# One-hot batches between the halves of the projections, expert tiles from pair 1, an eighth pair in 18 of 67 tiles

## What is computed

```python
xn = layernorm(x)
# state space: y = layernorm(xn)*gamma+beta; left, right = split(y @ W_up + b_up)
# left = silu(causal_conv3(left)); delta = softplus(left @ W_delta + b)
def step(h, inputs):
    u_t, d_t, b_t, c_t = inputs
    dA = jnp.exp(d_t[..., None] * A)
    h = dA * h + (d_t * u_t)[..., None] * b_t[:, None, :]
    y = jnp.einsum('bdn,bn->bd', h, c_t)
    return (h, y)
# s = xn + ((y + u*D) * silu(right)) @ W_down + b_down
# experts: the two best of 8 by xn @ gate, softmax over the two
# eo = (silu(xn @ w1) * (xn @ w3)) @ w2        (256 -> 1024 -> 256, for each expert)
# f = sum of the two experts' eo, weighted
out = x + s * silu(f)
```

## Time and profile before

| | us |
|---|---|
| runs | 1358.0, 1359.04, 1367.18; median 1359.04 |
| profiled execution | 1357.34, of which span 1355.5 |
| PE busy | 1189.3 (88%) |
| DVE busy | 1164.6 (86%) |
| POOL busy | 1076.8 (79%) |
| ACT busy | 756.1 (56%) |

### The profile page before, as it was taken

One profiled execution on the slowest core, in us unless ns is written; L12 is line 12 of the kernel. 1 busy time (PEld: TensorE's weight loads), 2 busy tenths in 40 slices (PEclk: granted clock), 3 DMA queues, 4 the chain that ended last, 5 costly groups with the idle time before them and its releaser, 6 DMA issues.

```text
span 1355.5 us, 26186 instructions
## 1 busy us (share of the span) xinstructions
PE 1189.3 (88%) x7740; PEld 916.5 (68%) x7740; DVE 1164.6 (86%) x1668; ACT 756.1 (56%) x1619; POOL 1076.8 (79%) x1044
## 2 busy tenths in 40 slices
PE   6767789999999999999889998999899989997850
PEld 5435577877777777777667876777687767775410
DVE  7726889989799888999888987998898979998988
ACT  3752475556655675566645664557555665555532
POOL 0032689889999889889988987899998888988974
PEclk7899799999999999999999999999999999997555
DMA  7114345564556545743474437444854476455658
GB/s 230 49 39 140 104 127 170 146 217 131 142 158 187 176 129 163 235 132 128 142 233 135 136 119 239 139 136 129 241 154 128 132 217 171 139 169 179 191 180 279
DMA packets 124319, 216.55 MB, mean 160 GB/s; under 512 B 15040, under 2 KB 40768, under 8 KB 124160
## 3 DMA queue, kind: packets, MB, share of 16 engines
q10 hardware_dynamic: 73728, 134.25, 34.0%
q1 hardware_dynamic: 43616, 61.83, 13.9%
q0 software_dynamic: 6816, 18.62, 4.3%
HBM read 190.67 MB, written 23.99 MB: 158 GB/s over the span
## 4 chain that ended last, share of the span: by engine, by line
PE 69%; POOL 9%; issue 8%; DMA 6%; DVE 5%; ACT 2%; SPq 0%; POOLq 0%; ACTq 0%; DVEq 0%
PE bank L1311 32%; PE bank L1281 15%; PE bank L1259 7%; PE bank L1325 7%; POOL arena L434 5%; DMA wring<-in_w_all 4%; PE bank L1166 2%; POOL hid L449 2%; PE bank L1188 1%; PE bank L1294 1%; PE bank L1196 1%; DVE arena L863 1%; PE bank L1268 1%; DVE xn L872 1%; DMA xg<-xn_d,source 1%
## 5 line engine op out<-in xcount | busy, mean ns | idle before, releaser
L434 POOL TENSOR_TENSOR arena<-arena,c_rep 128x512 f32<-128x512 f32 x512 | 604.2, 1185 | 113.0 <-DVE arena L1036 103.9
L1036 DVE TENSOR_TENSOR_SCAN arena<-bank,carry,arena 128x512 f32<-128x512 f32 x512 | 651.9, 1273 | 22.2 <-ACT bank L799 21.9
L1311 PEld LDWEIGHTS bank<-xgT,wring 128*128 128x128 f32 x4288 | 515.8, 193 | 134.9 <-issue 104.9
L1311 PE MATMUL bank<-xgT,wring 128*128 128x128 f32 x4288 | 536.3, 279 | 49.2 <-issue 29.0
L799 ACT ACTIVATE bank<-arena,a_neg 128x512 f32<-128x512 f32 x512 | 354.2, 692 | 122.1 <-DVE arena L1036 43.2
L1027 DVE TENSOR_TENSOR arena<-bank,b_rep 128x512 f32<-128x512 f32 x512 | 351.3, 686 | 32.5 <-PE bank L1325 11.2
L714 ACT ACTIVATE th<-bank 128x256 f32<-128x256 f32 x284 | 108.9, 384 | 339.0 <-PE bank L1311 303.9
L1325 PE MATMUL bank<-stack,pick 128*128 128x512 f32 x512 | 281.0, 550 | 17.0 <-DVE arena L1027 16.9
L1281 PE MATMUL bank<-wring,hid 128*128 128x256 f32 x1072 | 271.3, 386 | 8.6 <-POOL hid L449 8.5
L1281 PEld LDWEIGHTS bank<-wring,hid 128*128 128x128 f32 x1072 | 195.7, 191 | 63.1 <-issue 22.0
L449 POOL TENSOR_TENSOR hid<-gt,ue 128x256 f32<-128x256 f32 x284 | 207.0, 729 | 12.9 <-DVE gt L1048 12.7
(11 more groups left out here) (180 smaller groups left out, 772.9 us busy)
## 6 DMA issues: line engine op xcount, KB each, us to landing
arena<-delta_d ACTq DMA_DIRECT2D x512, 256.0 KB
wring<-in_w_all SPq DMA_DIRECT2D x64, 384.0 KB, 5.2
xn<-in_x SPq DMA_DIRECT2D x4, 1024.0 KB, 9.8
xn_d<-xn SPq DMA_DIRECT2D x4, 1024.0 KB, 5.5
parts_d<-spare SPq DMA_DIRECT2D x16, 256.0 KB
stack<-parts_d SPq DMA_DIRECT2D x16, 256.0 KB, 5.7
wring<-results SPq DMA_DIRECT2D x8, 512.0 KB, 9.1
arena<-results SPq DMA_DIRECT2D x8, 512.0 KB, 7.7
```

The lines of the kernel that those rows point to most:

```text
L434: pool.tensor_tensor(p_ring[:, s % P_RING, :], h_ring[:, s % H_RING, :], of_chunk(c_rep, c, 2), ALU.mult).then_inc(s_hc, 1)
L1036: v.tensor_tensor_scan(out=h_ring[:, s % H_RING, :], data0=a_bank[s % 2][:, :], data1=b_ring[:, s % B_RING, :], initial=carry[:, q:q + 1], ...
L1311: ins = pe.matmul(bank[:, m * SW + r * SLOT:m * SW + (r + 1) * SLOT], wring[:, 2 * j + r, (2 * m + h) * P:(2 * m + h + 1) * P], xgT[:, i % ...
```

## The change

The full batches and the shared ones are chosen by the list `SHARED` instead of every second; the batches are placed between and behind the two halves of each projection, from chunk 3 on, all of them before chunk 6 (batches 0 to 2 stand behind the products of chunk 0); transposes go one chunk ahead, and ACT's order follows. The destinations, the first gather and the first weight loads (in two parts) go ahead of the pairs. `yh`'s ring is turned round, so that the weights of the first four slots fit behind the rows that are used up first. Tiles start at pair 1; `EXTRA` spreads 18 pairs over the 67 live tiles; dead tiles take four pairs. They now stand at pairs 488 to 503.

```diff
-MOE_FIRST = 5
-PLACED_AT, GATHER_AT, WEIGHTS_AT = 1, 2, 1
+MOE_FIRST = 1
+SHARED = (1, 5, 7, 9, 11, 13, 15)
-LONG, SHORT = 7, 5
+LONG, SHORT, EXTRA = 7, 4, 18
...
-        first = MOE_FIRST + LONG * min(i, LONG_TILES) + SHORT * max(i - LONG_TILES, 0)
+        full = min(i, LONG_TILES)
+        first = MOE_FIRST + LONG * full + EXTRA * full // LONG_TILES + SHORT * (i - full)
...
+        def yh_row(c):
+            return (YH_RING - 1 - c % YH_RING) * TC
...
             load_stack(0)
+            sp.wait_ge(s_table, 1)
+            sp.wait_ge(s_ytr, YH_RING)
+            load_weights(0, (0, 1))
+            sp.wait_ge(s_ytr, NC)
+            load_weights(0, (2, 3))
...
-                if s == WEIGHTS_AT:
-                    sp.wait_ge(s_ytr, NC)
-                    sp.wait_ge(s_table, 1)
-                    load_weights(0, range(STEPS))
...
             gate_of_right(0)
+            pool.wait_ge(s_slot, 1)
+            values_of_halves(SHARED[0])
             for part in range(4):
                 delta_sum(0, part)
             low_part(0)
-            pool.wait_ge(s_slot, 1)
-            for b in range(1, BATCHES, 2):
+            for b in SHARED[1:]:
                 values_of_halves(b)
+            pool.wait_ge(s_placed, 5)
+            pool.wait_ge(s_xst, 16 * 4)
+            gather_rows(0)
...
+            evict_columns(3)
             evict_halves(2)
-            evict_columns(3)
             evict_c(0)
             scale_rows(4)
             high_part(0)
+            evict_columns(4)
+            scale_rows(5)
             evict_halves(3)
-            evict_columns(4)
-            for c in range(5, NC):
-                scale_rows(c)
-                evict_halves(c - 1)
-                evict_columns(c)
-            evict_halves(NC - 1)
+            for c in range(4, NC):
+                if c + 1 < NC:
+                    evict_columns(c + 1)
+                if c + 2 < NC:
+                    scale_rows(c + 2)
+                evict_halves(c)
...
-                if b % 2 == 0:
+                if b not in SHARED:
...
-            for b in range(BATCHES // 2):
+            for b in range(2):
                 one_hots(b)
...
-            for b in range(BATCHES // 2, BATCHES):
+            for b in range(2, BATCHES):
                 one_hots(b)
+            placed()
...
-            def left_right(c):
+            def left_right(c, between=()):
...
+                    if m == 0:
+                        for b in between:
+                            place_batch(b)
...
             product(0, "b")
+            place_batch(0)
             transpose_y(3)
             product(0, "c")
-            left_right(3)
-            placed_to = 0
-            for c in range(4, NC):
-                transpose_y(c)
-                left_right(c)
-                for b in range(placed_to, min(placed_to + 3, BATCHES)):
+            place_batch(1)
+            place_batch(2)
+            placed_to = 3
+            for c in range(3, NC):
+                if c + 1 < NC:
+                    transpose_y(c + 1)
+                left_right(c, range(placed_to, min(placed_to + 2, BATCHES)))
+                upto = min(placed_to + (5 if c == 5 else 4), BATCHES)
+                for b in range(placed_to + 2, upto):
                     place_batch(b)
-                placed_to += 3
-            for b in range(placed_to, BATCHES):
-                place_batch(b)
+                placed_to = upto
...
+                if s == 0:
+                    pe.wait_ge(s_lrev, NC - 1)
```

More of the change, by code:

```diff
@@ L410, in values_of_halves @@
             def values_of_halves(b):
-                pool.wait_ge(s_equal, b // 2 + 1)
+                pool.wait_ge(s_equal, SHARED.index(b) + 1)
                 shape = [P, BATCH, TILES]
@@ L415, in values_of_halves @@
                 pool.tensor_tensor(goals, weights, blocks(goal, b).unsqueeze(2).broadcast_to(shape), ALU.mult).then_inc(s_val, 1)
-                pool.wait_ge(s_val, 2 * (b // 2) + 1)
+                pool.wait_ge(s_val, 2 * SHARED.index(b) + 1)
                 pool.tensor_tensor(weights, weights, blocks(prob, b).unsqueeze(2).broadcast_to(shape), ALU.mult).then_inc(s_val, 1)
@@ L527, in _ @@
                     after_outs(BY_PAIR[s - 2])
-                if s == GATHER_AT:
-                    pool.wait_ge(s_placed, 5)
-                    pool.wait_ge(s_xst, 16 * 4)
-                    gather_rows(0)
                 for name, c, r in WORK[s]:
@@ L609, in scale_rows @@
                 for n in range(c * TC, (c + 1) * TC):
-                    ins = act.activation(yh[:, n % (YH_RING * TC), :], xn[:, n, :], ACT.Identity, scale=rs2[:, n:n + 1])
+                    ins = act.activation(yh[:, yh_row(c) + n % TC, :], xn[:, n, :], ACT.Identity, scale=rs2[:, n:n + 1])
                 ins.then_inc(s_yh, 1)
@@ L1069, in _ @@
                     gates(BY_PAIR[s - 1])
-                if s == PLACED_AT:
-                    placed()
                 c, at = s // PAIRS, s % PAIRS
@@ L1153, in transpose_y @@
                     pe.wait_ge(s_yev, c)
-                transpose_chunk(yh, (c % YH_RING) * TC, banks[0:2]).then_inc(s_ytr, 1)
-            def left_right(c):
+                transpose_chunk(yh, yh_row(c), banks[0:2]).then_inc(s_ytr, 1)
+            def left_right(c, between=()):
                 pe.wait_ge(s_yev, c + 1)
@@ L1192, in place_batch @@
                 pe.wait_ge(s_hot, b + 1)
-                if b % 2:
-                    pe.wait_ge(s_val, b + 1)
+                if b in SHARED:
+                    pe.wait_ge(s_val, 2 * SHARED.index(b) + 2)
                 for n in range(BATCH):
```

## The result

| | median of the runs, us | range | runs |
|---|---|---|---|
| before, on the chip of the comparison | 1358.52 | 1356.27 to 1367.18 | 4 |
| changed kernel | 1338.99 | 1337.68 to 1342.63 | 4 |

The ratio is 0.9853 with a 95% interval of 0.9822 to 0.9885: faster by 1.5%, where 2.2% had been forecast (1328). The time lies inside the range, and the sign is right. The profiled execution is the slowest of the four, 1342.63, with a span of 1340.8 against 1355.5.

The account below looks back on a forecast made before the run. PE and DVE, with nearly equal work, were taken to bound the loop by waiting for each other. Terms of -15.0, -4, -14.4, +1 and +3 sum to -29.4, from 1357.34 to 1328 us; range 1313 to 1345.

Parts of the forecast that it names:

- the eighth pair buys nothing: Rival for the loop: DVE paces the tiles, a light pair shortens nothing; 15 us less in all, 1342 us; chance 0.22.
- Head: Before the first scan: reordered one-hot batches end the last projection at 115.1, first scan at 120.5, 15.0 us earlier.
- First pairs: Start of the loop: destination operations and gather go ahead of it, under the last projections; 4 us less, bounds 0 and 5.
- Eighth pair: 18 live tiles: each moved pair without expert work saves 0.8 us, 14.4 us in all, bounds 0 and 24.
- Where DVE's floor is: Eight-pair tiles: DVE's work 16.4 us against PE's 15.3, so DVE becomes the floor; such tiles near 17.4 us.
- Dead tiles: Four-pair dead tiles: 3 us lost to POOL's lag, 2 won at the gather; net +1 us, bounds -4 and +6.
- Tail: After the last scan: result loads go out later, so POOL waits for the first chunk; +3 us, bounds 0 and +8.
- PE paces: Rival for the loop: every moved pair costs only 0.66 us, head near its good bound; 1314 us; chance 0.18.
- What would show it: Signs: first scan near 120 us, live tiles about 2.30 us a pair, clock 0.99, POOL waiting for the first results.

## Why the prediction was right or wrong

The forecast was 29.4 us less, the profiles show 14.7. The head's mechanism came, the largest term of the loop did not, and that the time still lies in the range is owed to a range that reaches over the rival in which the eighth pair buys nothing. Point by point:

- **Head, -15.0 forecast, -11.1 measured.** Right in kind. The step that failed is the durations of the one-hot batches, "I take 2.8" for a full one: batch 2 took 5.75 + 0.68 beside POOL's sums. The stepping also had no term for the clock, which fell while PE waited and cost 2.4 us behind it. Placement 2 ended at 81.1 and not at 76, and the lag stayed: 91.4 for 86.5, 100.6 for 95, 112.0 for 107 (batches 6, 10, 15). The last projection ended at 119.7 instead of 115.1. "I take 4.7" for the first exponential behind the last projection was near: 4.0. The forecast had a stretched row, 2.58 instead of 1.90, and took it for the worst case; it was a mild one. So the missing 4 us arise at one place, between 72 and 84 us. Moving batch 2 didn't help, as ACT's rows hold PE there until 78.0 anyhow; a kernel with both out of the way wasn't tried.
- **First pairs, -4 forecast, -2.4 measured.** The four pairs that went took 12.55 - 2.19 = 10.4 us with them, 2.4 more than 4 x 1.98. The rest of the 4 us was expected of pair 5, which "followed late as well"; no such gain shows.
- **Eighth pair, -14.4 forecast, -1.3 measured.** This is the error that matters. The 0.8 us saved on a moved pair can be had, and more: with the outputs out of the way it is 0.97 (twice) against the same kernel without eighth pairs, and with only the order turned the pair costs (1106.7 - 1093.3) / 18 = 0.74, so 1.24 are saved. What failed is the sentence "the number of pairs stays 512. What moves is where the pairs without expert work stand". More moved than that. The offsets of outputs are counted from a tile's start and reach beyond its end; a longer tile puts them on the next tile's step, ahead of it in PE's order. That costs 14.7 us of live stretch (1121.4 against 1106.7 with the order turned, nothing else changed). And the tiles begin four pairs earlier against the chunk work, which costs 8.4 us at seven pairs a tile. The second shows in three pairs of traces, 8.4, 5.9 without the later loads and some 8 with eighth pairs, and in the medians (7.7); its cause is not found. Of the 14.4 forecast, then: 18 x 1.24 = 22.3 saved, 6.2 lost against the kernel before by what else moved (469 pairs in 1093.3 and not 1087.1), 14.7 lost by the order, which leaves some 1.3 saved.
- **Where DVE's floor is.** The forecast said that in an eight-pair tile DVE becomes the floor, at about 17.4 us. No kernel came under 18.24. In the best one an eight-pair tile takes 18.39, 2.01 more than the same 17 tiles take without any eighth pairs (16.38), so at its own place the pair costs DVE's full price. The 17 tiles directly behind fell from 16.41 to 15.34, 18.0 us in all, the 32 others by 3.3 us together. The light pair is paid at once and pays back in the tile behind it. That this one catches up because other engines got ahead in the light pair is argued, and wasn't tried by itself.
- **Dead tiles, +1 forecast, -1.3 measured**, inside the bounds. Four-pair dead tiles cost no pace: 37.4 us for 16 pairs, 2.34 each as before (46.7 / 20 = 2.33). In the medians the kernel with them was 3.0 us slower than the one with five-pair tiles, by the ratios to the kernel before it was equal (0.9860 and 0.9861).
- **Tail, +3 forecast, +1.5 measured.** The mechanism is there, in POOL's timeline of the changed kernel:

```profile
1294.13 1.01 POOL L460 DMA_INDIRECT results<-o_sb,dest  x1
...
1302.34 2.34 POOL L557 TENSOR_TENSOR wring<-wring 128x1024 f32<-128x1024 f32 x1
...
1306.03 2.35 POOL L557 TENSOR_TENSOR wring<-wring 128x1024 f32<-128x1024 f32 x1 [1.34 <-DMA wring<-results]
```

The first chunk was there in time, the second came 1.34 us late.

- **Rivals.** "The eighth pair buys nothing", 1342, is what the time says (1339), but not for its reason: DVE's pace and the weights did not forbid the gain, as the kernel with the order turned shows, at 1326.7 on the forecast's 1328. "PE paces" (1314) did not come, although with the right order the pair's price of 0.74 is near its 0.66. The clock stayed at 0.98 to 0.99 in the loop, so no fall behind the light pairs shows.
- **What would show it.** The pace of 2.30 us a pair in the live stretch came (1121.4 / 487), and it proved nothing: at that pace the eighth pair had cost what it saved. The number that should have been set down is the pace against the kernel without eighth pairs.

## What to carry to other kernels

In an order written out by hand, with offsets counted from a tile's start, a longer or shifted tile changes more than its own length: write down, for each boundary, what now stands ahead of what on the busiest in-order engine, and whether it waits. Put the instruction that starts a chain (here the next tile's step, with tanh, copy and gate behind it) ahead of one that ends a chain (the last outputs), even where that one doesn't wait: its own 1.8 us are what the chain loses. Turning 18 such pairs round was worth 12.3 us in the medians, against 9.6 for the eighth pairs themselves. And a change of two halves should be timed in halves: here one half was the whole gain and the other hid a gain and a loss of nearly the same size. And before a stall is taken out, look for a second chain that ends just before it: in the head it left 0.7 us of a stall of 5.56.

## What the runs showed of the hardware

DVE's small operations beside POOL's elementwise sums stretch far beyond the 2.58 instead of 1.90 of the earlier trace rows. Eight compares of 128 x 71 took 5.75 us instead of 1.90 while POOL ran four sums of 128 x 512. In the trace's single records four of the eight took 1.26 to 1.30 us, each ending within 0.1 us after a sum, and the four between them their usual 0.30 to 0.31: each sum held one compare. With batch 2 moved, three operations of 0.20 to 0.23 us took 1.19, 1.31 and 1.34, again each ending with a sum of 1.27 (76.29, 77.64, 78.98 against 76.35, 77.69, 79.07). It also goes the other way: the sum ahead of these took 2.20 us, while DVE's operations of 128 x 512 and 128 x 568 beside it took their usual 0.69 and 0.75.

The Trainium skill ("GPSIMD Engine Reference", Specifications) says that GpSimd shares its SBUF interfaces with VectorE and contends with DVE instructions in a 2-port mode or with two SBUF inputs. The trace agrees that the two hold each other up: three times the time for the eight compares, six times for the shortest operations. Which of these instructions ran in such a mode no run here shows.

Second, TensorE's clock fell when PE had waited 5.56 us in the head: the granted clock was 0.50, the 1.2 GHz level, from 78 to 82 us, and the eight matmuls of a placement took 2.26 us instead of 1.13. In the loop, a step behind a wait of 3.24 us still took 2.02 us; the next one in that trace, at 838.91 behind a wait of 3.29, took 2.65, and the window from 840 to 845 shows 0.66.

Third, the loads of the seven later experts cost 24.7 us of live stretch from pair 1 and 22.2 from pair 5, while PE's waits under their name are 22.9 and 15.7. Here a wait that was taken away was worth more than its row says, and not by a fixed share.
